# The first layer's recurrence: from Toeplitz matmuls to chunks of 32 tokens with a carried state

## The reference

```python
h = _rmsnorm(x, norm_w)
u = h @ Win + b_in
u = conv(u, conv_w, causal, 4 taps, one filter per channel) + conv_b
def step(hc, u_t):
    hc = einsum('bdr,drs->bds', hc, A) + u_t[:, :, None] * Bv[None]
    y = einsum('bds,ds->bd', hc, Cv)
...
return y @ Wout + b_out + res
```

## Time and profile before

| | us |
|---|---|
| median of 3 runs | 2436.68 (2435.02 to 2443.68) |
| profiled execution | 2446.33 |
| its span | 2444.6 |
| `load_x` | 0 to 59 |
| `kernels` | 59 to 190 |
| `recurrence` | 190 to 445.7 |
| `project` | 445.7 to 561.5 |
| everything behind | 561.5 to 2444.6 |

### The profile page before, as it was taken

How to read it: one execution, slowest core, us unless ns; L and a number is a source line. 1 busy time by engine, 2 the same in 40 slices (tenths; PEclk the granted TensorE clock), 3 DMA queues, 4 the chain that set the end, 5 groups by cost and what they waited for, 6 DMA issues and landing times. The chain is left out here.

```text
span 2444.6 us, 31503 instructions
## 1 busy us (share of the span) xinstructions
PE 1734.2 (71%) x9106; PEld 1310.7 (54%) x9106; DVE 1528.8 (63%) x3384; ACT 1033.7 (42%) x1728; POOL 827.6 (34%) x717
## 2 busy tenths in 40 slices
PE   2903455666999999999577757767779994443599
PEld 2903355434777777777355535545546663222387
DVE  6787422355766666666546757767765566988566
ACT  0308400224544555554345635543447772222454
POOL 2020000002555555555300005530038783222255
PEclk9955565777999999999757758878879997665699
DMA  1001488106755555545100006430011111000355
GB/s 37 13 9 62 145 279 288 63 11 140 152 111 110 113 113 110 115 108 109 42 18 1 1 6 122 104 80 1 1 27 43 34 34 26 0 1 1 69 121 120
DMA packets 144435, 179.55 MB, mean 73 GB/s; under 512 B 37527, under 2 KB 89051, under 8 KB 144379
## 3 DMA queue, kind: packets, MB, share of 16 engines
q1 hardware_dynamic: 142568, 178.47, 30.5%
q10 hardware_dynamic: 1810, 0.42, 0.1%
HBM read 174.53 MB, written 4.33 MB: 73 GB/s over the span
## 5 line engine op out<-in xcount | busy, mean ns | idle before, releaser
L794 POOL TENSOR_TENSOR ffn_alo<-ffn_a,ffn_ahi 128x512 fp32r<-128x512 f32 x520 | 669.6, 1290 | 509.3 <-ACT ffn_ahi L755 505.6
L821 DVE TENSOR_TENSOR ffn_a<-ffn_G,ffn_mask 128x512 f32<-128x512 f32 x384 | 264.8, 690 | 241.6 <-ACT ffn_G L763 218.6
L763 ACT ACTIVATE ffn_G<-ffn_G 128x512 f32<-128x512 f32 x384 | 223.5, 582 | 359.0 <-PE ffn_G L104 356.9
L755 ACT ACTIVATE ffn_ahi<-ffn_a 128x512 fp32r<-128x512 f32 x520 | 324.7, 624 | 32.9 <-DVE ffn_a L825 29.0
L102 PE MATMUL ypsum<-ffn_ahi,ffn_hi 128*128 128x512 f32 x520 | 228.1, 439 | 48.7 <-POOL ffn_alo L794 34.9
L102 PE MATMUL ffn_G<-xn_hi,ffn_hi 128*128 (+1 forms) x520 | 220.8, 425 | 31.3 <-DVE ffn_lo L801 27.5
L825 DVE TENSOR_TENSOR ffn_a<-ffn_U,ffn_a 128x512 f32<-128x512 f32 x320 | 221.4, 692 | 29.7 <-DVE ffn_a L821 0.5
L194 POOL TENSOR_TENSOR ln_var<-ln_moments,eps 128x4 f32<-128x4 f32 x56 | 11.1, 199 | 671.2 <-DVE ln_moments L174 671.2
L103 PE MATMUL ffn_G<-xn_lo,ffn_hi 128*128 (+1 forms) x520 | 214.4, 412 | 0.0
L104 PE MATMUL ffn_G<-xn_hi,ffn_lo 128*128 (+1 forms) x520 | 213.8, 411 | 0.0
L103 PE MATMUL ypsum<-ffn_alo,ffn_hi 128*128 128x512 f32 x520 | 210.6, 405 | 0.0
(11 more groups left out here) (509 smaller groups left out, 3788.0 us busy)
## 6 DMA issues: line engine op xcount, KB each, us to landing
ffn_mask<-mask_rows_top SPq DMA_DIRECT2D x128, 512.0 KB, 6.8
rec_T<-scratch_kernels SPq DMA_DIRECT2D x32, 1536.0 KB, 7.7
ffn_mask<-mask_rows_top SPq DMA_DIRECT2D x16, 1024.0 KB, 8.2
ffn_mask<-mask_rows_zone SPq DMA_DIRECT2D x16, 1024.0 KB, 8.3
ffn_mask<-mask_rows_steps SPq DMA_DIRECT2D x16, 512.0 KB, 4.7
x<-in_L_attn_x SPq DMA_DIRECT2D x8, 256.0 KB, 4.8
ffn_raw<-in_L_ffn_expert_gate_k SPq DMA_DIRECT2D x16, 128.0 KB, 3.3
ffn_raw<-in_L_ffn_expert_up_k SPq DMA_DIRECT2D x16, 128.0 KB, 3.4
```

The lines of the kernel that those rows point to most:

```text
L755: act.activation(ahi[i][:, :], a[i][:, :], ACT.Copy).then_inc(k.ahi_done, 1)
L763: act.activation(gate if masked(c) else a[c % RING_A][:, :], gate, how, **kw).then_inc(k.r_done, 1)
L794: eng.tensor_tensor(alo[i][:, :], a[i][:, :], ahi[i][:, :].bitcast(F32), ALU.subtract).then_inc(k.alo_done, 1)
L821: dve.tensor_tensor(out, gate[:, :], mask(c), ALU.mult).then_inc(k.t_done, 1)
```

## The change

One block (`Scan`, and the five functions beginning with `scan_`) takes the place of blocks 1 to 3, and block 4 is cut down. What it computes:

- Each matrix of 8 channels is squared side by side with its vectors. Round `n` takes three of the 32 matrices at one of 5 levels: the moving operand is the matrix with the vectors found so far behind it (`A` with C·A^j in columns 128 on, `AT` with A^j·B), 129 to 144 columns, so that a level doubles the vectors too: 1, 2, 4, 8, 16, 32 of them. In the last level one of the two products is the 16 new columns alone. There are 55 rounds. The norm of x (statistics on DVE in the first 8 rounds, a scaled copy on ACT, transposes on PE from round 22 on, `hi` on ACT, `lo` on DVE) is laid between the rounds.
- `cbd`: the first 32 numbers of each channel's answer, 16-partition rows sent to HBM and read back as Toeplitz blocks of 32x32 (four transfers, `T0c`), which POOL spreads over block diagonals `T0`.
- U with the four taps inside: 128 tokens at a time (the same place j of the 128 chunks), 4 taps x 3 = 12 fp32r matmuls of 256 columns for each of 32 places, 384 in all; the stationary operand is `x[:, j-m:TOKENS:CHUNK]`, features by every 32nd token. DVE adds the bias and writes U in another order. Between them are 64 transposes of the expanded A^j·B (`E`, to `G`).
- U is turned (64), multiplied by `G` to what each chunk adds to the state (64 matmuls of 112 columns), then the state is carried over six steps of 32 matmuls with 16 columns, one column per sequence, DVE adding each (L2230, L2463). The output is `U2`·`T0` plus `H`·`F` (128 matmuls of 128 columns), copied, turned (64 transposes), and copied again with a step of 32 elements.
- `project`: neither transposes nor bias matmuls; `Wout` is applied one turn earlier, and the bias comes with a later copy on ACT. 10 turns.

The core of the diff (all lines are new; the old functions stand above):

```diff
+def scan_loads(k, s, block):
...
+        sp.wait_ge(ev["k_out"], 32)
+        sp.wait_ge(ev["zero_out"], 16)
+        sp.wait_ge(ev["u_psum"], 8)
+        for c in range(QUAD):
+            src = bass.AP(s.rows.tensor, c * 2 * CHUNK + 1, [[1, CHUNK], [QUAD * 2 * CHUNK, UNITS], [1, CHUNK]])
+            sp.dma_start(s.T0c[CHUNK * c:CHUNK * (c + 1), :, :], src).then_inc(ev["t0_in"], 16)
...
+def scan_tensor(k, s, block):
...
+        def norm(g):
+            pe.wait_ge(ev["h_done"], g + 1)
+            if g >= 2:
+                pe.wait_ge(ev["lo"], g - 1)
+            for j in range(GT):
+                last = pe.transpose(turn[g % 2][:, j * P:(j + 1) * P], s.h[g % 2][:, j, :], k.ident[:, :])
+            last.then_inc(ev["turned"], 1)
+        for n in range(ROUNDS):
+            level, t = divmod(n, TRIS)
+            if n >= LN_TURN and (n - LN_TURN) % 2 == 0 and (n - LN_TURN) // 2 < GROUPS:
+                norm((n - LN_TURN) // 2)
+            if level == 0:
+                pe.wait_ge(ev["at_copied"], (min(3 * t + 3, PACKS) - 1) // 4 + 1)
+                if 1 <= n < 3:
+                    pe.wait_ge(ev["at_copied"], 2 * n + 4)
+            else:
+                evicted(n - TRIS)
+            if n >= 3:
+                evicted(n - 3)
+            more = 1 << level
+            b0, b1 = bank[2 * (n % 3)], bank[2 * (n % 3) + 1]
+            for i, p in enumerate(range(PACKS)[trio(t)]):
+                at = 160 * i
+                if level < LEVELS - 1:
+                    pe.matmul(b0[:, at:at + P + more], A[:, p, 0:P], AT[:, p, 0:P + more], start=True, stop=True)
+                else:
+                    pe.matmul(b0[:, at + P:at + P + more], A[:, p, 0:P], AT[:, p, P:P + more], start=True, stop=True)
+                last = pe.matmul(b1[:, at:at + P + more], AT[:, p, 0:P], A[:, p, 0:P + more], start=True, stop=True)
+            last.then_inc(ev["squared"], 1)
...
+        pe.wait_ge(ev["lo"], GROUPS)
+        for p in range(PACKS):
+            last = pe.matmul(k.turn[:, p:p + 1], A[:, p, 0:P], AT[:, p, P:P + 1], start=True, stop=True)
+        last.then_inc(ev["l32_psum"], 1)
+        pe.wait_ge(ev["cbd"], 1)
+        for p in range(PACKS):
+            out = (k.ypsum, bank[4])[p // 16]
+            last = pe.matmul(out[0:PACK, p % 16 * CHUNK:(p % 16 + 1) * CHUNK], s.cbd[:, p, :], AT[:, p, P:P + CHUNK],
+                             start=True, stop=True)
+            if p % 16 == 15:
+                last.then_inc(ev["k_psum"], 1)
+        pe.wait_ge(ev["win_done"], 1)
+        pe.wait_ge(ev["shifted"], 1)
+        for i in range(8):
+            if i >= 2:
+                pe.wait_ge(ev["u_done"], i - 1)
+            for at in range(4):
+                j = 4 * i + 3 - at
+                for m in range(TAPS):
+                    if j >= m:
+                        x = [t[:, j - m:TOKENS:CHUNK] for t in (k.xh, k.xl)]
+                    else:
+                        x = [t[:, m - j - 1, :] for t in s.before]
+                    last = mm3(pe, s.wide[i % 2][:, at * CH:(at + 1) * CH], *x, s.win_hi[:, m, :],
+                               s.win_lo[:, m, :], start=(m == 0), stop=(m == TAPS - 1))
+            last.then_inc(ev["u_psum"], 1)
+            for e in (2 * i, 2 * i + 1):
+                pe.wait_ge(ev["e_pool" if e % 2 else "e_dve"], e // 2 + 1)
+                if e == 0:
+                    pe.wait_ge(ev["k_copied"], 2)
+                if e >= 2:
+                    pe.wait_ge(ev["g_copied"], e - 1)
+                for v in range(4):
+                    last = pe.transpose(bank[4 + e % 2][:, v * P:(v + 1) * P],
+                                        s.E[e % E_RING].rearrange("p g c j -> p (g c j)")[:, v * P:(v + 1) * P],
+                                        k.ident[:, :])
+                last.then_inc(ev["g_turned"], 1)
...
+        for r in range(16):
+            turn_u(r)
+            if r >= 4 and r % 2 == 0:
+                state((r - 4) // 2)
+        for q in range(6, 8):
+            state(q)
+        pe.wait_ge(ev["v_done"], 8)
+        pe.wait_ge(ev["u2_done"], 16)
+        for n in range(1, CHUNKS - 1):
+            for sub in range(SUBS):
+                if n > 1:
+                    pe.wait_ge(ev["sc_done"], SUBS * (n - 2) + sub + 1)
+                out = (bank[3], bank[4], bank[5], k.turn)[sub]
+                for i in range(8):
+                    p = 8 * sub + i
+                    last = pe.matmul(out[:, i * BATCH:(i + 1) * BATCH], A[:, p, 0:P], s.H[:, p, n:P:CHUNKS],
+                                     start=True, stop=True)
+                last.then_inc(ev["sc_psum"], 1)
+        for r in range(16):
+            if r == 0:
+                pe.wait_ge(ev["h_zero"], 1)
+                pe.wait_ge(ev["sc_done"], SUBS * (CHUNKS - 2))
+            pe.wait_ge(ev["t0_done"], r + 1)
+            pe.wait_ge(ev["f_done"], r + 1)
+            if r >= 4:
+                pe.wait_ge(ev["y_dve" if r % 2 else "y_act"], (r - 4) // 2 + 1)
+            out = (bank[0], bank[1], bank[2], k.ypsum)[r % 4]
+            for i in range(2):
+                p = 2 * r + i
+                for half in range(2):
+                    at = i * 2 * P + half * P
+                    pe.matmul(out[:, at:at + P], s.U2[:, 2 * p + half, :],
+                              s.T0[:, 2 * p + half, :, :].rearrange("p c j -> p (c j)"), start=True, stop=False)
+                    last = pe.matmul(out[:, at:at + P], s.H[:, p, :],
+                                     s.F[:, p, QUAD * half:QUAD * (half + 1), :].rearrange("p c j -> p (c j)"),
+                                     start=False, stop=True)
+            last.then_inc(ev["y_psum"], 1)
+        for r in range(16):
+            t, first = r // 8, r % 8 * 4
+            pe.wait_ge(ev["y_act"], 4 * t + 4)
+            pe.wait_ge(ev["y_dve"], 4 * t + 4)
+            if r >= 4:
+                pe.wait_ge(ev["yc_dve" if r % 2 else "yc_act"], (r - 4) // 2 + 1)
+            out = (bank[3], bank[4], bank[5], k.turn)[r % 4]
+            for i in range(4):
+                last = pe.transpose(out[:, i * P:(i + 1) * P], s.Y[t][:, :, first + i], k.ident[:, :])
+            last.then_inc(ev["yt_turned"], 1)
...
+def scan_vector(k, s, block):
...
+        for n in range(ROUNDS):
+            level, t = divmod(n, TRIS)
+            more = 1 << level
+            dve.wait_ge(ev["squared"], n + 1)
+            b1 = bank[2 * (n % 3) + 1]
+            dve.tensor_copy(A[:, trio(t), P + more:P + 2 * more], slots(b1, t, P, more))
+            dve.tensor_copy(A[:, trio(t), 0:P], slots(b1, t, 0, P)).then_inc(ev["a_copied"], 1)
+            if n < GROUPS:
+                stats(n)
+            if n == GROUPS:
+                aggregate()
+            if n == GROUPS + 2:
+                weights()
+            if n == GROUPS + 7:
+                blocks()
+            g, odd = divmod(n - LN_REST, 2)
+            if 0 <= g < GROUPS and not odd:
+                rest(g)
...
+        for n in range(1, CHUNKS - 1):
+            for sub in range(SUBS):
+                dve.wait_ge(ev["sc_psum"], SUBS * (n - 1) + sub + 1)
+                out = (bank[3], bank[4], bank[5], k.turn)[sub]
+                h = s.H[:, 8 * sub:8 * sub + 8, n + 1:P:CHUNKS]
+                dve.tensor_tensor(h, h, out[:, 0:8 * BATCH].rearrange("p (g b) -> p g b", b=BATCH), ALU.add)\
+                   .then_inc(ev["sc_done"], 1)
+                if f < PAIRS:
+                    dve.tensor_tensor(s.F[:, 2 * f:2 * f + 2, :, :],
+                                      A[:, 2 * f:2 * f + 2, P:P + CHUNK].unsqueeze(2).to_broadcast([P, 2, PACK, CHUNK]),
+                                      s.mask8.unsqueeze(1).unsqueeze(3).to_broadcast([P, 2, PACK, CHUNK]), ALU.mult)\
+                       .then_inc(ev["f_done"], 1)
+                    f += 1
...
+def scan_gpsimd(k, s, block):
...
+        pool.wait_ge(ev["t0_in"], 64)
+        pool.wait_ge(ev["ut_turned"], 16)
+        for r in range(16):
+            pool.tensor_tensor(s.T0[:, 4 * r:4 * r + 4, :, :],
+                               s.T0c[:, 4 * r:4 * r + 4, :].unsqueeze(2).to_broadcast([P, 4, QUAD, CHUNK]),
+                               s.mask4[:, :].unsqueeze(1).unsqueeze(3).to_broadcast([P, 4, QUAD, CHUNK]), ALU.mult)\
+                .then_inc(ev["t0_done"], 1)
...
 def project(k, s, next_route):
...
+                def output(g):
+                    if g:
+                        pe.wait_ge(k.y_copied, base + g)
+                    for t in range(CT):
+                        last = pe.matmul(k.ypsum[:, :], s.wout[:, t, :], s.yc[:, t, g * GROUP:(g + 1) * GROUP],
+                                         start=(t == 0), stop=(t == CT - 1))
+                    last.then_inc(k.y_done, 1)
...
+                for g in turns:
+                    p = Pipeline(g, g, g)
+                    p.part(2, post, 7)
+                    p.part(1, post, 1)
+                    p.part(0, output)
+                    p.part(2, post, 9)
```

(45 more changed lines are left out.)

807 lines of the change are left out of this document (376 added, 431 removed).

## The result

The changed kernel takes 2340.81 us (median of 4 runs, 2336.39 to 2346.43) against 2440.18 for the kernel before (4 runs, 2435.02 to 2455.22): ratio 0.9605, 95% interval 0.9573 to 0.9637. Faster, as forecast, but 33 us above the forecast of 2308. It is inside the stated range of 2250 to 2350 only by the piece that the strided rival had added: the likeliest case's own bounds ended at 2335. The profiled execution took 2336.39, its span is 2334.7, the mean granted clock 0.844. The projection begins at 349.3 us (327 was predicted, 445.7 before) and ends at 461.9.

A forecast was written before the change was run, and what follows sets the result against it. Old bound: latency, then ACT, then transfers; new: PE's time plus its waits. Block 445.7 to 327.4 saves 118.3, projection 11: profiled 2446.33 to 2317.0; profiled execution 9.65 over the median, so 2308, range 2250 to 2350.

The forecast's parts named there:

- the strided rival: In U: every strided weight load costs 1.47 times, adding 15 of 45 us, total 2323; chance 0.08.
- the likeliest case: Whole kernel: the forecast itself, 2308 us, with its own bounds giving 2290 to 2335; chance 0.62.
- stayed hidden, as said: Beside the new block: T0, bias chain, F blocks and Toeplitz reads (estimated at 10 us) cost nothing.
- the term of U: In the new block: 384 fp32r matmuls at 0.117 us, 64 transposes and 2 for waits, 54.6 us.
- by the row, nothing, and the sum goes by the row: In U: stationary operands read at 128-byte steps add nothing, since transposes of ssm_Y at that step take 0.12 each.
- The largest unknown: Carried state: 192 narrow f32 matmuls at half clock, 0.455 us each, 86.4 us; rival at full clock, 2262, chance 0.22.
- 0.236 for full clock: Carried state: time per narrow matmul at full clock, 192 of them 45.3 us.
- 11 for 3.2: Projection: output moved ahead, transposes and bias matmuls gone, 1.5 to 2 us a turn over seven turns; 11 saved (3 to 16).
- less what the longer front part gives back: Projection: a deduction from the seven turns' gain of 1.5 to 2 us each, leaving 11.
- the 5 us for DVE: In the squaring: DVE's copies and statistics slower than PE in 11 early rounds, +5 us.
- the 3 for ACT: In the squaring: ACT's four more scaled copies in the 16 rounds with the norm, +3 us.
- the term of A^32·B: In the new block: last power 11 us, first 32 numbers' matmuls 4, two copies 1; 16 us.

The follow-up runs named there:

- e8: Changed kernel with e1, e2, e5 and 128 columns in the last power's matmuls: 2244.28 us, ratio 0.9226.
- e1: Changed kernel with the normed x written so that U's stationary operands are read straight: 2295.58 us, ratio 0.9433.
- e4: Changed kernel, U's taps reading weights at steps of 1, 2, 4, 32 elements, state's f32 matmuls at 128 bytes: U matmuls 0.11 to 0.12 or 0.23 us apart.
- e6: Changed kernel, carried-state matmuls reading 16 columns side by side instead of every 8th (other numbers than wanted): carried state 80 to 81 us.
- e7: As e2 against the changed kernel, but 64 columns per carried-state matmul (other numbers than wanted): carried state 80 to 81 us.
- e2: Changed kernel with 128 columns instead of 16 in the carried state's matmuls, in eight banks: 2297.84 us, ratio 0.9461.
- e5: Changed kernel with the projection's output product issued between the routing's transposes and the turned norm: 2331.14 us, ratio 0.9566.
- e12: Changed kernel in e5's order, with one Wout matmul instead of two (half the product left out): projection 108.0 us.
- e11: Changed kernel in its own order, with one Wout matmul instead of two (half the product left out): projection 108.0 us.
- e9: Changed kernel with all eight maskings of A on DVE instead of four on DVE, four on POOL: projection begins at 347.1 us, first squaring 13.2.

## Why the prediction was right, and where it was wrong

**Direction and most terms.** The block became one chain of PE work; start, squaring, first numbers, state, outputs were within 6 us each. T0, the bias chain, F and the Toeplitz reads stayed hidden, as said. In e8, where the carried state is 37 us shorter, they still do. That the time fell inside the range has luck in it: U was 37.4 us too long, and the other terms of the block together 15.5 too short. Had they come out as predicted, the time would have been about 2356, above the range.

**The step that failed is in the term of U: "by the row, nothing, and the sum goes by the row".** It went by the earlier trace rows, transposes of `ssm_Y` at 128 bytes and 0.12 apart, and gave the rival 0.08, priced at 15. (Its own ratio gives more: 0.47 of 44.9 is 21, and so do its 0.17 apart.) The cost is 0.11 for each of 366 matmuls, 40 us (e1: 92.0 to 51.4), more than the whole excess of 33. The Trainium skill ("SBUF — State Buffer", Door 1) says that each access to a new 16-byte line pays; e4 agrees for matmuls, with the edge between two and four elements, while the spacing of the transposes does not. Two things were wrong in the reading of rows. First, a transpose was taken for a matmul. In the changed kernel the load of a stepped transpose (L2262) is busy 193 ns where a straight one (L2182) is 141, and the transposes are still 0.11 apart. In an fp32r matmul of 256 columns the load is 318 against 197, and the matmuls are 0.22 apart instead of 0.11. Why a stepped load is slower in a matmul than in a transpose was not tested; the number of columns does not explain it, since e4's f32 matmuls of 112 columns pay too, with loads of 311. Second, the price came from DVE reading at 64 bytes (1.47 times); on PE it is 2.0 times.

**The largest unknown was right.** The carried state ran at half clock with PE never idle: 80.6 predicted as 86.4, at 0.42 per matmul, not 0.455. (The prediction's 0.236 for full clock is no row's number either; 0.91 for four is 0.228. The sum does not use it.) e6 and e7 show that the stride of the moving operand is not the cause, and e2 that 128 columns are at full clock. The rule that the gate follows how busy PE is (the Trainium skill, "TensorE: Matmul & The Clock Gate", Part 1) would have had full clock here, if busy is read as in the profile, where PE has 80.06 of 80.60 us. The trace does not agree with it in that reading.

**The projection was over-estimated, 11 for 3.2.** The turns did not get shorter at all: six of them (L155 to L155, 364.0 to 439.3) took 12.5 us each, where L149 to L149 (465.7 to 539.5) had taken 12.3. The 3.2 us were gained ahead of them, from the stage's start to the second L155: 14.7 us where it had been 20.0. The term took the gap between the turned norm and the routing weights in two turns and counted the difference as gained, "less what the longer front part gives back". Two things gave it back. The first is the order: L333 stands behind the output, DVE's routing comes later, and PE idles 2.2 to 3.0 us ahead of L338. So from L155 to L338 a turn still takes 9.4 us, where it had been 10.1, and not 1.5 to 2 less. The second is a term that the prediction left out, the granted clock: the projection had 0.77 and has 0.67. From L338 to the next L155 six turns took 3.2 us on average, 2.2 before. One such stretch before and one after the change, the same seven matmuls (four transposes of the routing weights, three products with the router's weights) at either level:

```profile
475.90:478.10 2.20, 1.43 (x9) 0.96 (x8) 0.00 (x0) 1.07 (x2) 0.00 (x0) 1.00 0.00 0
```

```profile
398.30:401.50 3.20, 2.43 (x7) 1.57 (x8) 0.52 (x1) 0.59 (x1) 0.00 (x0) 0.50 0.12 28
```

With the best place of the output (e5) 107.8 us are left, and with half an output too (e12). My second theory, that this place would give 25, failed since idle time of PE on either side of a wait for DVE is one slack, not two: in e5, e11 and e12 L338 comes 8.7 us after L155 whatever PE does between. That DVE sets this part is shown by e5, e11 and e12; how much of the 108 us the lower clock is was not isolated.

**Small terms.** The squaring needed neither the 5 us for DVE nor the 3 for ACT: PE idled 2.6 us there, once, for DVE. In the term of A^32·B two errors cancel: the last power took 13.3 us at half clock, not 11, and the 32 columns of the first numbers 3.5, not 5. The split masks (e9) explain more than the 1.2 that the start was late.

## What to carry to other kernels

Before a tile is read as a stationary operand, look at the step in bytes of its inner dimension: a copy that writes it straight was dearer in itself but hidden here, and saved 40 us. Where a long stretch is made of narrow matmuls, look at its granted clock, and try the full width: here the unwanted columns cost nothing and halved the stretch; with 64 of the 128 it stayed as it was. A wait of PE for DVE is not filled twice: find whose chain sets the turn by halving PE's part, before its order is changed, and compare the granted clocks when you do.

## What the runs showed of the hardware

- A matmul whose stationary operand is read at steps of 4 or 32 elements of 4 bytes takes twice as long as one at 1 or 2, for fp32r (0.23 and 0.11 to 0.12 us with 256 columns), and so does an f32 one at 32 against straight (0.44 and 0.22 with 112 columns). Transposes at 32 do not: 0.11 apart.
- 192 f32 matmuls in a row, with PE hardly idle: with 16 or 64 columns each 80 to 81 us at a granted clock of 0.51, with 128 columns 43.4 us at 1.00.
- DVE was slower beside POOL in the masking: 1486 ns, and 684 alone.
- Writes at steps of 512 bytes cost DVE 1050 ns instead of 680 and ACT 1138 instead of 591 for 128x512 (e1), hidden behind PE.
